# Reordering the queries, the scores and the FFN scaling in a fused Perceiver block: first the second half of the queries, then scores and scaling in alternation

## The chip, the cores and the metric

The kernel runs on one core of one Trainium2 chip. The metric is the device time of one execution in microseconds (us); the median of several executions counts. The work is spread over TensorE (PE in the profile, its weight loads PEld), VectorE (DVE), ScalarE (ACT), GpSimd (POOL) and SyncE (SP, which here only issues transfers). Each engine works through its own instructions in the order in which they are written and waits on semaphores for what other engines produce.

## What is computed

The reference takes `x` (16 x 64 x 1024) and a context (16 x 1024 x 1024) through three stages, each with a residual sum:

```python
x = x + matmul(fake_quant(layernorm(x)), fake_quant(ctx_4096))     # 1: quantized product
x = x + attention(layernorm(x), Wqkv, Wo)    # 2: 32 query heads of 32, one k/v head, ALiBi, causal
x = x + ffn(layernorm(x), weight, bias, gate_w, in_channel_scale, out_channel_scale)   # 3

# attention
scores = jnp.einsum('bqhd,bkd->bhqk', q, k) * scale
probs = softmax(where(causal, scores + alibi, NEG_INF))
attn = jnp.einsum('bhqk,bkd->bqhd', probs, v) @ Wo
# ffn
routing = softmax(xf @ gate_w.T)
in_scale, out_scale = routing @ in_channel_scale, routing @ out_channel_scale
out = xf * in_scale @ sign(weight).T * out_scale + bias
```

## The kernel before

The 1024 rows of `x` are cut into eight tiles of 128 rows, each of which holds two batches of 64 rows. The three stages overlap between tiles: in step i, TensorE works on stage 1 of tile i+1, the queries and scores of tile i, the attention product and projection of tile i-1, and the FFN of tile i-1 and then i-2. The whole order is written out by hand, engine by engine, in `first_half(s)` and `second_half(s)`, which `run_steps` calls for each step (L132). `s.front` (f), `s.middle` (m) and `s.next` (n) say which tiles exist in a step. Steps 2 to 7 run through the code that the change touches with f and m both true; step 8 has no tile in front.

Products that need precision beyond float16 are made from a high and a low part: ACT makes the high part (`hi_part`), DVE the low part (`lo_part`), and TensorE adds three products. These functions matter here:

- `query(s, n, ks)` on PE makes half n of the transposed queries, 12 matmuls for each k in `ks`; `low` and `high` are k 0 to 3 and 4 to 7. When the last k of half 1 is done, ACT runs `q_hi(s, 1)` and DVE then `q_lo(s, 1)` (writes qT_lo, L830).
- `scores(s, b)` on PE (L1393, 24 matmuls for each batch b) waits for both `q_lo`. DVE's `scores_in(t, h, b)` (L982) scales one 128x512 block of them, adds ALiBi and writes `Pr`; `row_max` (L987) and `subtract_max` (L316) follow. For b = 1 the subtraction is on POOL, for b = 0 on DVE. The first four of these calls were the function `softmax_in`, at the end of the second half; the rest, `softmax_rest`, begins the next step's first half with `scores_in(m, 1, 0)`.
- The router's weights come out of `router_probs` (DVE) through `router_t` (PE, L1467) and `rt_copy` (ACT). `inscale(s, c)` (PE, L1479, 4 matmuls each) spreads them over half c of the channels. DVE's `xs(s, c)` (L1068) multiplies the FFN's input by them, ACT's `xs_hi` and DVE's `xs_lo` (XS_lo, L828) split it.
- `context(t, pair)` on PE (L1308) is a quarter of stage 1: 8 matmuls with a branch (L1318) in their middle.
- `outscale(s, n)` (PE, L1496) opens the FFN's half in the next step. Its guards are the waits

```python
emptied(Step(s.i - 1), f"is{n}")                  # xs_lo(n) of the step before is done
e.wait_ge(s_stt, (s.i - 1) * 4 + 2 + n)           # n=0: two scores_in are done, n=1: three
```

so that `outscale(s, 0)` needs `xs_lo(0)` and `scores_in(0, 1)`, and `outscale(s, 1)` needs `xs_lo(1)` and `scores_in(1, 0)`. `ffn(s, n, ks)` (L1504) follows each. ACT's `outscale_copy` (L554) waits for `outscale(s, 1)`; behind it on ACT stand the exponentials `exp` (L548), for which the transposes `pt` (PE, L1327) wait.

Of the kernel before, what the change touches and what calls it, by code (L numbers as in the profile page):

```python
# [145 lines left out]
def build(nc, x, context, wqkv, wo, w_t, bias, quant_in, small_in, scales_in, alibi, out):  # L146
    ctx = ExitStack()
    with ctx:
# [672 lines left out]
        def _(e):  # L821
# [241 lines left out]
            def xs(s, c):  # L1063

                m, bank, sl = s.i - 1, s.bank(f"is{c}"), slice(4 * c, 4 * c + 4)
                e.wait_ge(s_is, m * 2 + c + 1)
                rows = ln2T[:, sl, :].rearrange("p k t -> p (k t)")
                e.scalar_tensor_tensor(rows, T[:, bank, :], C_XS, rows, ALU.mult, ALU.mult)\  # L1068
                    .then_inc(s_xs, 1)

            def xs_lo(s, c):
                m, bank, sl = s.i - 1, s.bank(f"is{c}"), slice(4 * c, 4 * c + 4)
                e.wait_ge(s_xshi, m * 2 + c + 1)
                lo_part(XS[1][:, sl, :], ln2T[:, sl, :], XS[0][:, sl, :], 1.0, s_free[bank])
# [10 lines left out]
            def softmax_in(m):  # L1085

                scores_in(m, 0, 0)
                scores_in(m, 0, 1)
                row_max(m, 0, 0)
                subtract_max(e, m, 0, 0)  # L1090
# [32 lines left out]
            def entry():  # L1123
                stats0(0)
                norm0(0, tok)
                stats0(1)
                norm0(1, tok)
                scales_by_part()
# [72 lines left out]
            def second_half(s):  # L1201
                f, m, n = s.front, s.middle, s.next
                if s.is_step(-1):
                    return entry()
                if s.is_step(0):
                    return step_0(s)
                if s.is_step(1):
                    return step_1(s, Step(2))
                if f and not s.is_step(2):
                    x1(s)  # L1210
                if m and not s.is_step(2):
                    ta_lo(s, 1)
                if f and not s.is_step(2):
                    norm1(s)
                if n and not s.is_step(2):
                    stats0(s.i + 1)
                if m and not s.is_step(2):
                    x2(s, 0)
                if f and not s.is_step(2):
                    t1_lo(s, 0)  # L1220
                    t1_lo(s, 1)
                if m and not s.is_step(2):
                    x2(s, 1)
                if f:
                    v_lo(s)

                def second_norm():
                    if m:
                        norm2(s)

                if n and not s.is_step(2):
                    norm0(s.i + 1, tok, second_norm)
                else:
                    second_norm()
                if f:
                    q_lo(s, 0)
                    k_lo(s)
                if m:
                    router_max(s)
                    router_probs(s)  # L1240
                if m:
                    xs(s, 0)
                    xs(s, 1)
                if f:
                    q_lo(s, 1)
                if m:
                    xs_lo(s, 0)
                    xs_lo(s, 1)
                if f:
                    softmax_in(s.i)  # L1250

            run_steps(first_half, second_half)

# [2 lines left out]
        def _(e):  # L1256
# [5 lines left out]
            low, high = range(KT // 2), range(KT // 2, KT)  # L1262
# [27 lines left out]
            def context(t, pair, s=None):  # L1290


                if pair == 0:
                    if t < 2:
                        emptied(s, "T0")
                    else:
                        e.wait_ge(s_aT, 16 * (t - 1))
                    if t == 2:
                        e.wait_ge(s_x2, 2)
                    at_least(e, s_k, t)  # L1300
                    at_least(e, s_v, t)
                c = 2 * pair + 1
                e.wait_ge(s_rf[c % RING], uses(t, c) + 1)

                def products(k, lhs, first, last):
                    for n in range(2):
                        for b in range(2):
                            ins = e.matmul(C[b * S:(b + 1) * S, n, :], lhs(b),  # L1308
                                           b16[:, (2 * pair + b) % BRING, k, n * HALF:(n + 1) * HALF],
                                           start=first, stop=last)  # L1310
                    return ins

                def rows(k):
                    return lambda b: aT[:, 2 * pair + k, b * S:(b + 1) * S]

                products(0, rows(0), pair == 0, False)

                with e.If_ne(uneven, 0):  # L1318
                    for k in range(2):
                        for part in range(3):  # L1320
                            products(k, lambda b: zfrac[:, part, :], False, False)
                products(1, rows(1), False, pair == 3).then_inc(s_ctx, 1)
# [27 lines left out]
            def query(s, n, ks=range(KT)):  # L1350

                if n == 0 and k_low(ks):
                    if s.is_step(1):
                        e.wait_ge(s_k, 2)
                        e.wait_ge(s_v, 2)
                    else:
                        at_least(e, s_an, s.i * 4)
                if s.is_step(2) and k_low(ks):
                    e.wait_ge(s_fe, n + 1)
                for k in ks:  # L1360
                    rows = [t[:, k, :].rearrange("p (b t) -> p b t", b=2) for t in T16]
                    for g in range(4):
                        dst = query_to(s.i, n).rearrange("p (b g t) -> p g b t", b=2, t=S)[:, g]
                        at = (4 * n + g) * P
                        hi, lo = (w[:, k, at:at + P] for w in Wqkv)
                        e.matmul(dst, hi, rows[0], start=k == 0 and g == 0, stop=False,  # L1366
                                 skip_group_check=True)
                        e.matmul(dst, hi, rows[1], start=False, stop=False, skip_group_check=True)  # L1368
                        last = e.matmul(dst, lo, rows[0], start=False, stop=k == KT - 1,  # L1369
                                        skip_group_check=True)  # L1370
                if ks[-1] == KT - 1:
                    last.then_inc(s_qT, 1)
# [98 lines left out]
            def inscale(s, c):  # L1471
                bank = bank_for(s, f"is{c}")
                if c == 0:
                    emptied(s, "rT")
                    if s.is_step(1):
                        e.wait_ge(s_prep, 3)
                for k in range(4):
                    at = (4 * c + k) * P
                    last = e.matmul(T[:, bank, k * P:(k + 1) * P], insc[:, at:at + P], rT[:, :],  # L1479
                                    start=True, stop=True)  # L1480
                last.then_inc(s_is, 1)
# [143 lines left out]
            def second_half(s):  # L1625
                f, m, n = s.front, s.middle, s.next
                if s.is_step(-1):
                    return entry(s)
                if s.is_step(0):
                    return step_0(s)  # L1630
                if s.is_step(1):
                    return step_1(s, Step(2))
                if f and not s.is_step(2):
                    t1(s)
                if m and not s.is_step(2):
                    project(s, 1, high)
                if f:
                    kv(s)
                    query(s, 0)
                if m:  # L1640
                    t2(s)
                if f:
                    query(s, 1, low[:1])
                    tk(s)
                    query(s, 1, low[1:])
                if m:
                    router(s)
                if f:
                    query(s, 1, high[:2])
                if n:  # L1650
                    context(s.i + 1, 0, s)
                if m:
                    router_t(s)
                if f:
                    query(s, 1, high[2:3])
                if m:
                    inscale(s, 0)
                    inscale(s, 1)
                if f:
                    query(s, 1, high[3:])  # L1660
                if n:
                    context(s.i + 1, 1)
                if f:
                    scores(s, 0)
                    scores(s, 1)
# [45 lines left out]
```

## Time and profile before

| | |
|---|---|
| runs of the kernel | 442.26, 444.58 and 444.25 us, median 444.25 us |
| profiled execution | 442.26 us, of which the span from first to last instruction is 440.5 us |
| PE busy | 373.2 us (85%) |
| DVE busy | 309.6 us (70%) |
| ACT busy | 257.3 us (58%) |
| POOL busy | 96.2 us (22%) |

A busy share alone doesn't say which engine bounds the kernel: the shares are means over a start-up of some 110 us in which transfers count, six steps that repeat, and a tail with little left to overlap. The rows below come from the repeating steps, where the changed lines run.

### The profile page before, as it was taken

How to read it: one execution, taken by the hardware profiler on the slowest of the kernel's cores; microseconds unless marked ns; L12 is line 12 of the kernel's file. 1: busy time of each engine (PE TensorE's matmuls, PEld its weight loads, DVE VectorE, ACT ScalarE, POOL GpSimd, SP SyncE). 2: the span in 40 equal slices, each digit the busy share in tenths (PEclk: the TensorE clock that was granted, in tenths of full speed). 3: DMA queues.
4: the chain of work that ended last, by engine and by line, in shares of the span. 5: the costliest groups of instructions: out<-in, count | busy, mean ns of one | idle time of the engine just before them, and what ended most of it. 6: DMA issues, size and time to landing. Idle time of an engine off the chain costs nothing.

```text
span 440.5 us, 9600 instructions
## 1 busy us (share of the span) xinstructions
PE 373.2 (85%) x3952; PEld 255.0 (58%) x3952; DVE 309.6 (70%) x586; ACT 257.3 (58%) x308; POOL 96.2 (22%) x116
## 2 busy tenths in 40 slices
PE   0444956996999999998999999989999999899565
PEld 0114835953636956694659655965587558755432
DVE  7668579989846387787688688858786865483331
ACT  4777898747678655764666576756577523241110
POOL 5210010003503203140314041403231312031202
PEclk9955997999899999999999999999999999999759
DMA  7999998699399864777277736774591010001001
GB/s 313 390 399 409 409 378 325 241 361 357 134 388 305 285 235 136 258 235 251 76 283 243 218 131 254 270 217 144 199 328 25 1 49 2 3 1 49 0 0 48
DMA packets 30097, 91.97 MB, mean 209 GB/s; under 512 B 8224, under 2 KB 8224, under 8 KB 30048
## 3 DMA queue, kind: packets, MB, share of 16 engines
q1 hardware_dynamic: 27888, 83.40, 53.5%
q10 hardware_dynamic: 2160, 7.87, 4.8%
q8 instruction: 37, 0.61, 0.5%
q14 instruction: 12, 0.10, 0.1%
HBM read 85.50 MB, written 4.19 MB: 204 GB/s over the span
## 4 chain that ended last, share of the span: by engine, by line
PE 65%; DVE 11%; DMA 9%; ACT 5%; issue 4%; SPq 3%; POOL 0%; POOLq 0%; DVEq 0%; ACTq 0%
PE R L1504 13%; PE T L1327 7%; PE R L1278 7%; DMA ring<-ctx 7%; PE R L1280 6%; PE R L1279 6%; PE C L1308 5%; PE R L1366 4%; PE R L1369 4%; PE R L1368 4%; ACT b L524 3%; PE T L1460 3%; SPq L348 2%; PE R L1393 2%; DVE st L878 1%
## 5 line engine op out<-in xcount | busy, mean ns | idle before, releaser
L524 ACT ACTIVATE b<-ring,quant,qpar 128x2048 uint8<-128x2048 f32 x64 | 133.0, 2091 | 10.7 <-DMA ring<-ctx 7.9
L1366 PE MATMUL R<-T_hi,Wqkv_hi 128*128 128x128 f16 x448 | 78.6, 221 | 0.0
L1368 PE MATMUL R<-T_lo,Wqkv_hi 128*128 128x128 f16 x448 | 78.5, 221 | 0.0
L1369 PE MATMUL R<-T_hi,Wqkv_lo 128*128 128x128 f16 x448 | 78.4, 221 | 0.0
L1504 PE MATMUL R<-sgn,XS_hi 128*128 128x512 fp8e4 x128 | 49.7, 388 | 0.0
L1308 PE MATMUL C<-b,aT 128*64 128x512 f16 x256 | 37.2, 416 | 14.5 <-ACT b L524 10.7
L1504 PE MATMUL R<-sgn,XS_lo 128*128 128x512 fp8e4 x128 | 49.4, 386 | 0.0
L1366 PEld LDWEIGHTS R<-T_hi,Wqkv_hi 128*128 128x128 f16 x448 | 44.8, 100 | 1.0
L1368 PEld LDWEIGHTS R<-T_lo,Wqkv_hi 128*128 128x128 f16 x448 | 44.2, 99 | 0.1
L1369 PEld LDWEIGHTS R<-T_hi,Wqkv_lo 128*128 128x128 f16 x448 | 44.3, 99 | 0.0
L316 POOL TENSOR_TENSOR Pr<-Pr,mx 128x512 f32<-128x512 f32 x16 | 16.7, 1044 | 125.2 <-DVE mx L987 125.2
L1278 PE MATMUL R<-Wo,attT_hi 128*128 128x512 f16 x112 | 43.0, 384 | 0.5 <-DVE attT_lo L1013 0.5
L1279 PE MATMUL R<-Wo,attT_hi 128*128 128x512 f16 x112 | 42.7, 381 | 0.0
L1280 PE MATMUL R<-Wo,attT_lo 128*128 128x512 f16 x112 | 42.7, 381 | 0.0
L878 DVE BATCH_NORM_STATS2 st<-X 128x6 f32<-128x512 f32 x48 | 33.3, 693 | 4.0 <-DMA X<-x 2.5
L425 POOL TENSOR_TENSOR small<-small,consts 128x1 f32<-128x1 f32 x24 | 4.6, 192 | 134.2 <-DVE small L885 134.2
L448 POOL TENSOR_TENSOR X<-X,XL 128x512 f32<-128x512 f32 x16 | 20.3, 1271 | 48.7 <-DVE XL L1082 48.7
L1327 PE MATMUL T<-ident,XL 128*128 128x128 f32 x120 | 19.3, 314 | 12.1 <-DVE XL L890 12.1
L1308 PEld LDWEIGHTS C<-b,aT 128*64 128x64 f16 x256 | 12.4, 115 | 28.6 <-ACT b L524 13.7
L573 ACT ACTIVATE attT_hi<-T 128x512 f16<-128x512 f32 x16 | 9.5, 594 | 31.6 <-PE T L1327 31.6
L828 DVE TENSOR_TENSOR PT_lo<-T,PT_hi 128x512 f16<-128x512 f32 x32 | 20.6, 684 | 8.6 <-ACT PT_hi L508 8.6
L1327 PEld LDWEIGHTS T<-ident,XL 128*128 128x128 f32 x120 | 16.0, 163 | 14.9 <-DVE XL L890 13.7
(145 smaller groups left out, 873.1 us busy)
## 6 DMA issues: line engine op xcount, KB each, us to landing
ring<-ctx SPq DMA_DIRECT2D x64, 1024.0 KB, 6.2
ring<-L_attn_Wo SPq DMA_DIRECT2D x4, 1024.0 KB, 7.6
ring<-L_ffn_weight SPq DMA_DIRECT2D x4, 1024.0 KB, 5.0
out<-X ACTq DMA_DIRECT2D x8, 512.0 KB, 2.6
Wo<-L_attn_Wqkv SPq DMA_DIRECT2D x7, 544.0 KB, 15.1
X<-x ACTq DMA_DIRECT2D x7, 512.0 KB, 4.0
sgn<-L_attn_Wqkv SPq DMA_DIRECT2D x1, 544.0 KB, 18.1
X<-x SPq DMA_DIRECT2D x1, 512.0 KB, 12.8
```

The costliest lines, as they stand in the source:

```text
L524: e.activation(b8[:, c % BRING, :], ring[:, slot, :], ACT.Identity, scale=qR2, bias=qZ2).then_inc(s_rf[slot], 1)
L828: e.tensor_tensor(dst, src, hi, ALU.subtract).then_inc(done, 1)
L878: link(e.bn_stats(st[k][:, h, :], src[:, h * HALF:(h + 1) * HALF]))
L1278: e.matmul(dst, lhs[0], rhs[0], start=first, stop=False)
L1279: e.matmul(dst, lhs[0], rhs[1], start=False, stop=False)
L1280: return e.matmul(dst, lhs[1], rhs[0], start=False, stop=last)
L1308: ins = e.matmul(C[b * S:(b + 1) * S, n, :], lhs(b), b16[:, (2 * pair + b) % BRING, k, n * HALF:(n + 1) * HALF], start=first, stop=last)
L1327: last = e.transpose(T[:, bank, n * P:(n + 1) * P], src, ident[:, :])
L1366: e.matmul(dst, hi, rows[0], start=k == 0 and g == 0, stop=False, skip_group_check=True)
L1368: e.matmul(dst, hi, rows[1], start=False, stop=False, skip_group_check=True)
L1369: last = e.matmul(dst, lo, rows[0], start=False, stop=k == KT - 1, skip_group_check=True)
L1504: last = e.matmul(R[:, 2 + n, :], XS[part][:, k, :], sgn[:, k, n * HALF:(n + 1) * HALF], start=k == 0 and part == 0, stop=k == KT - 1 and ...
```

## The change

On DVE, in the second half of a step, `q_lo(s, 1)` moves ahead of both `xs`, and the calls of `xs`, `xs_lo` and the four of `softmax_in` are put in alternation. On PE the last query group is joined to the one before it, so that it runs ahead of `inscale`, and `context(s.i + 1, 1)` goes between the two `inscale`. No instruction is added or taken away, and ACT, POOL and SP keep their order.

```diff
@@ DVE, second_half
                 if m:
                     router_max(s)
                     router_probs(s)
+                if f:
+                    q_lo(s, 1)
                 if m:
                     xs(s, 0)
+                if f:
+                    scores_in(s.i, 0, 0)
+                if m:
                     xs(s, 1)
                 if f:
-                    q_lo(s, 1)
+                    scores_in(s.i, 0, 1)
                 if m:
                     xs_lo(s, 0)
+                if f:
+                    row_max(s.i, 0, 0)
+                if m:
                     xs_lo(s, 1)
                 if f:
-                    softmax_in(s.i)
+                    subtract_max(e, s.i, 0, 0)
@@ PE, second_half
                 if m:
                     router_t(s)
                 if f:
-                    query(s, 1, high[2:3])
+                    query(s, 1, high[2:])
                 if m:
                     inscale(s, 0)
-                    inscale(s, 1)
-                if f:
-                    query(s, 1, high[3:])
                 if n:
                     context(s.i + 1, 1)
+                if m:
+                    inscale(s, 1)
                 if f:
                     scores(s, 0)
                     scores(s, 1)
```

On DVE, from the end of the router's work in step 3 up to the third `scores_in` of the next half, the kernel before has (ln2T is written by `xs`, qT_lo by `q_lo`, XS_lo by `xs_lo`, Pr<-R by `scores_in`, mx by `row_max`, Pr<-Pr by `subtract_max`):

```order
L1060 TENSOR_TENSOR rstack<-rt,rstack 128x16
L1068 SCALAR_TENSOR_TENSOR ln2T<-T,ln2T 128x512 x2
L830 SCALAR_TENSOR_TENSOR qT_lo<-R,qT_hi 128x2x256
L828 TENSOR_TENSOR XS_lo<-ln2T,XS_hi 128x512 x2
L982 SCALAR_TENSOR_TENSOR Pr<-R,alibi_sb 128x512 x2
L987 TENSOR_REDUCE mx<-Pr 128x8
L316 TENSOR_TENSOR Pr<-Pr,mx 128x512
L982 SCALAR_TENSOR_TENSOR Pr<-R,alibi_sb 128x512
```

On DVE at the same place the changed kernel has:

```order
L1060 TENSOR_TENSOR rstack<-rt,rstack 128x16
L830 SCALAR_TENSOR_TENSOR qT_lo<-R,qT_hi 128x2x256
L1068 SCALAR_TENSOR_TENSOR ln2T<-T,ln2T 128x512
L982 SCALAR_TENSOR_TENSOR Pr<-R,alibi_sb 128x512
L1068 SCALAR_TENSOR_TENSOR ln2T<-T,ln2T 128x512
L982 SCALAR_TENSOR_TENSOR Pr<-R,alibi_sb 128x512
L828 TENSOR_TENSOR XS_lo<-ln2T,XS_hi 128x512
L987 TENSOR_REDUCE mx<-Pr 128x8
L828 TENSOR_TENSOR XS_lo<-ln2T,XS_hi 128x512
L316 TENSOR_TENSOR Pr<-Pr,mx 128x512
L982 SCALAR_TENSOR_TENSOR Pr<-R,alibi_sb 128x512
```

The two `xs` now stand behind `q_lo`, and the first `xs_lo` behind both `scores_in` of the first pair, while it stood ahead of them.

On PE the kernel before has, from the last matmuls of the query's last group in step 3 to the first of the scores (a branch leaps over the row of 24):

```order
L1368 MATMUL R<-T_lo,Wqkv_hi 128x2x64
L1369 MATMUL R<-T_hi,Wqkv_lo 128x2x64
L1308 MATMUL C<-b,aT 64x512 x4
L1318 COMPARE_AND_BRANCH
L1308 MATMUL C<-b,zfrac 64x512 x24
L1318 UNCONDITIONAL_BRANCH
L1308 MATMUL C<-b,aT 64x512 x4
L1393 MATMUL R<-kbd_hi,qT_hi 128x128 x2
```

On PE the changed kernel has there (its lines stand 8 lower in the file; L1487 is `inscale`, L1401 the scores):

```order
L1376 MATMUL R<-T_lo,Wqkv_hi 128x2x64
L1377 MATMUL R<-T_hi,Wqkv_lo 128x2x64
L1487 MATMUL T<-rT,scales 128x128 x4
L1316 MATMUL C<-b,aT 64x512 x4
L1326 COMPARE_AND_BRANCH
L1316 MATMUL C<-b,zfrac 64x512 x24
L1326 UNCONDITIONAL_BRANCH
L1316 MATMUL C<-b,aT 64x512 x4
L1487 MATMUL T<-rT,scales 128x128 x4
L1401 MATMUL R<-kbd_hi,qT_hi 128x128 x2
```

The eight matmuls of `inscale`, which stood together ahead of the query's last group, now follow it, four on each side of the context group.

## Rows read from the trace of the kernel before

**Rows 1.** The page, part 1: busy us (share of the span) and instructions by engine.

```profile
PE 373.2 (85%) x3952; PEld 255.0 (58%) x3952; DVE 309.6 (70%) x586; ACT 257.3 (58%) x308; POOL 96.2 (22%) x116
```

**Rows 2.** Windows: stretch, length, busy us by engine, granted clock, DMA share, GB/s.

```profile
154.32:199.19 44.87, 44.17 (x495) 30.64 (x493) 35.89 (x69) 28.69 (x37) 11.62 (x12) 1.00 0.65 219
199.19:245.13 45.94, 44.35 (x495) 30.53 (x493) 35.89 (x69) 28.68 (x37) 11.61 (x12) 1.00 0.63 212
...
384.15:390.00 5.85, 4.92 (x63) 2.71 (x64) 5.82 (x10) 1.06 (x2) 0.96 (x1) 1.00 0.02 4
```

**Rows 3.** Timeline, PE, step 4: start us, us, engine, line, tiles, [idle before].

```profile
246.07 0.61 PE L1479 MATMUL T<-rT,scales 32*128 32x128 f16 x8
246.62 0.23 PE L1366 MATMUL R<-T_hi,Wqkv_hi 128*128 128x128 f16 x1
...
247.24 0.22 PE L1369 MATMUL R<-T_hi,Wqkv_lo 128*128 128x128 f16 x1
247.39 0.41 PE L1308 MATMUL C<-b,aT 128*64 128x512 f16 x2
...
248.92 0.23 PE L1393 MATMUL R<-kbd_hi,qT_hi 64*128 64x128 f16 x2 [0.47 <-issue]
...
250.37 0.41 PE L1308 MATMUL C<-b,aT 128*64 128x512 f16 x2
...
251.36 0.37 PE L1496 MATMUL R<-scales,rT 32*128 32x512 f16 x1
...
253.50 0.39 PE L1496 MATMUL R<-scales,rT 32*128 32x512 f16 x1
...
255.56 0.51 PE L1327 MATMUL T<-ident,Pr 128*128 128x128 f32 x3
```

**Rows 4.** Timeline, DVE, the same stretch of step 4.

```profile
248.13 0.69 DVE L830 SCALAR_TENSOR_TENSOR qT_lo<-R,qT_hi 128x512 f16<-128x512 f32 x1 [0.34 <-ACT qT_hi L508]
248.73 1.28 DVE L828 TENSOR_TENSOR XS_lo<-ln2T,XS_hi 128x512 f16<-128x512 f32 x2
...
249.93 1.28 DVE L982 SCALAR_TENSOR_TENSOR Pr<-R,alibi_sb 128x512 f32<-128x512 f32 x2
...
252.45 0.69 DVE L982 SCALAR_TENSOR_TENSOR Pr<-R,alibi_sb 128x512 f32<-128x512 f32 x1
```

**Rows 5.** Timeline, ACT and then POOL, the same stretch.

```profile
247.50 0.60 ACT L508 ACTIVATE qT_hi<-R 128x512 f16<-128x512 f32 x1 [1.76 <-PE R L1369]
...
253.92 1.02 ACT L554 ACTIVATE XL<-R 128x1024 f32<-128x1024 f32 x1 [2.81 <-PE R L1496]
254.84 1.14 ACT L548 ACTIVATE Pr<-Pr 128x512 f32<-128x512 f32 x2
...
253.81 1.04 POOL L316 TENSOR_TENSOR Pr<-Pr,mx 128x512 f32<-128x512 f32 x1 [11.37 <-DVE mx L987]
```

**Rows 6.** Timeline, step 0: first scores on PE, first `scores_in` on DVE.

```profile
56.28 0.23 PE L1393 MATMUL R<-kbd_hi,qT_hi 64*128 64x128 f16 x2 [1.50 <-DVE qT_lo L830]
...
57.17 0.69 DVE L982 SCALAR_TENSOR_TENSOR Pr<-R,alibi_sb 128x512 f32<-128x512 f32 x1 [0.24 <-PE R L1393]
```

**Rows 7.** Timeline, PE and then DVE, step 7, which has no context product.

```profile
384.15 0.23 PE L1393 MATMUL R<-kbd_hi,qT_hi 64*128 64x128 f16 x2 [1.46 <-issue]
...
386.60 0.37 PE L1496 MATMUL R<-scales,rT 32*128 32x512 f16 x1 [0.93 <-DVE Pr L982]
...
385.17 1.28 DVE L982 SCALAR_TENSOR_TENSOR Pr<-R,alibi_sb 128x512 f32<-128x512 f32 x2
```

**Rows 8.** Timeline, PE, step 3, and the branches of that stretch (durations in ns).

```profile
205.93 0.62 PE L1308 MATMUL C<-b,aT 128*64 128x512 f16 x4 [0.88 <-issue]
...
208.63 0.39 PE L1496 MATMUL R<-scales,rT 32*128 32x512 f16 x1
...
L1318 PEldq COMPARE_BRANCH  x3: 205/207/2022, 197.4 to 203.9; - x3
```

**Rows 9.** Timeline, PE, step 5: first context product after the transposing transfer.

```profile
289.96 0.41 PE L1308 MATMUL C<-b,aT 128*64 128x512 f16 x2 [0.88 <-DMA aT<-a]
```

More of the change, by code:

```diff
@@ L1240, in second_half @@
                     router_probs(s)
-                if m:
-                    xs(s, 0)
-                    xs(s, 1)
                 if f:
@@ L1246, in second_half @@
                 if m:
+                    xs(s, 0)
+                if f:
+                    scores_in(s.i, 0, 0)
+                if m:
+                    xs(s, 1)
+                if f:
+                    scores_in(s.i, 0, 1)
+                if m:
                     xs_lo(s, 0)
+                if f:
+                    row_max(s.i, 0, 0)
+                if m:
                     xs_lo(s, 1)
                 if f:
-                    softmax_in(s.i)
+                    subtract_max(e, s.i, 0, 0)
             run_steps(first_half, second_half)
@@ L1654, in second_half @@
                 if f:
-                    query(s, 1, high[2:3])
+                    query(s, 1, high[2:])
                 if m:
                     inscale(s, 0)
-                    inscale(s, 1)
-                if f:
-                    query(s, 1, high[3:])
                 if n:
                     context(s.i + 1, 1)
+                if m:
+                    inscale(s, 1)
                 if f:
```

## The prediction, made before the changed kernel was run

> **What bounds the kernel now.** I read the page's busy shares first: PE 85%, the next engine 70% [rows 1]. A mean doesn't name a limit, so I cut the trace into stretches from one `router_t` to the next. In step 2 to 3 PE is busy 44.17 of 44.87 us at a granted clock of 1.00, that is its upper level of 2.4 GHz, and DVE 35.89 [rows 2]. So in the repeating steps TensorE sets the pace, and a change counts only by what it does to the moments at which PE waits. The timeline of PE shows them for step 4 [rows 3]: the only sizeable one is the 0.47 us before the scores at 248.92. The other thing to see is where PE is almost late for nothing. `outscale(0)` starts at 251.36, just as the context group before it (0.99 us from 250.37) runs out, but DVE's second `scores_in`, which it also needs, ends at 249.93 + 1.28 = 251.21 [rows 3, 4]. That guard is 0.15 us from costing something. In step 7, where there is no context group between, the same guard does bite: 0.93 us of idle PE before `outscale(0)`, released by DVE [rows 7]. The guard of `outscale(1)` (the third `scores_in`, end 252.45 + 0.69 = 253.14) has 0.36 us to its start at 253.50 [rows 3, 4]. DVE is thus a second, nearly equal chain between the queries' end and `outscale(1)`, and the change lengthens exactly that chain.
>
> **Part 1, PE: the queries end earlier.** The last twelve matmuls no longer wait behind eight of `inscale`, which take 246.62 - 246.07 = 0.55 us with their step over to the query; joining two groups of twelve also saves a step over: (247.24 - 246.62)/11 = 0.056 us for one, 0.68 us for twelve, against 247.39 - 246.62 = 0.77 with the change of group [rows 3]. I take 0.55 + 0.1 = 0.65 us in all. `q_hi` follows on ACT (idle for 1.76 us before it, so free), then `q_lo` on DVE, 248.13 before [rows 4, 5]; DVE is idle there too, since `xs` now stands behind. So `q_lo` starts at 247.47 and ends at 248.16. PE has the same work as before between router and scores and arrives without a wait at 248.92 - 0.47 - 0.1 = about 248.3. Of the wait at the scores nothing is left: a gain of 0.6 to 0.65 us in each of six steps, 3.8 us if nothing else moved. In step 7, PE still waits (1.46 us before, about 1.0 now), and also starts the scores 0.65 us earlier [rows 7].
>
> **Part 2, DVE: the chain behind `q_lo`.** Before, both `xs` ran in the time in which DVE waited for `q_hi`. That time was their cover, and it is gone: DVE now waits idle for `q_hi`, and 2 x 0.60 us of work comes after. One such instruction behind another starts 0.60 us later (two of XS_lo: 248.73 to 249.93) [rows 4]. The first `scores_in` also has to wait for all 24 matmuls of batch 0; in step 0, where DVE really waited for them, it started 57.17 - 56.28 = 0.89 us after the first of them [rows 6]. Now the chain of step 4, by starts: `q_lo` 247.47, `xs(0)` 248.07, then idle until 248.3 + 0.89 = 249.2, `scores_in(0,0)` 249.2, `xs(1)` 249.8, `scores_in(0,1)` 250.4, `xs_lo(0)` 251.0, `row_max` 251.6, `xs_lo(1)` 252.2, `subtract_max` 252.8, and the next half's `scores_in(1,0)` 253.4, which ends at 254.08. ACT's two `xs_hi` (0.6 us each) fit between: each has over 1.2 us from the end of its `xs` to its `xs_lo`.
>
> **Part 3, the guards.** `outscale(0)` now waits for `xs_lo(0)`, which ends at 251.0 + 0.68 = 251.68; with the 0.15 us that DVE's end takes to reach PE (386.45 to 386.60 in step 7, where 386.45 is two `scores_in` behind 385.17) it starts at 251.8, where it started at 251.36. PE itself would be there at 250.7, so it idles 1.1 us. `outscale(1)` would follow 253.50 - 251.36 = 2.14 us later [rows 3], at 253.97, but its guard opens at 254.08 + 0.15 = 254.2: 0.7 us later than 253.50. So the 0.65 us won at the scores are already inside this number, and the step stands 0.7 us behind.
>
> **Who waits behind it.** Behind `outscale(1)`, PE has eight matmuls and then the transpose `pt` at 255.56, which the exponential of 254.84 released (first half ends about 255.46) [rows 3, 5]. ACT's copy and exponentials start at `outscale(1)` + 0.42, and shift by the same 0.7. The subtraction on POOL ended at 254.85 and was needed at 255.36; it shifts by 0.95 (with `scores_in(1,0)`, 252.45 to 253.4) against 0.7, and keeps 0.25 us. ACT's conversion behind `xs_hi(1)` runs some 2 us later, into time in which ACT idled 2.81 us [rows 5]. Ring slots come free as much later, with loads that a whole step separates from their use. In the whole of the stretch from step 2 to 3 PE is idle for 44.87 - 44.17 = 0.70 us [rows 2], and two thirds of that are the wait at the scores; what is left for the other forty microseconds is some 0.2 us, and DVE's and ACT's work there starts from PE's. So nothing gives the 0.7 back. Even the wait for the transposing transfer in step 5 (0.88 us) [rows 9] stays: its source is made by DVE behind PE's work of the same step.
>
> **Sum.** Steps 2, 4, 5, 6 and 7 look alike; step 7 by its own rows: `outscale(1)` at 388.73 becomes 389.4. That is 5 x 0.7 = 3.5 us. Step 3 is different. There PE lost 0.88 us inside the context group at 205.93, on a branch that took 2022 ns where others take 207 [rows 8], and `outscale(1)` stood at 208.63. DVE's chain there is step 4's less 45.94 us, the time from one `router_t` to the next [rows 2], so its guard opens at 254.2 - 45.94 = 208.3, and the branch's loss falls into the new idle time: a gain of 0.35 us. Total 3.5 - 0.35 = +3.1 us. Against the profiled execution, 442.26 us (1.76 us of it outside the span), that is 445.4. That execution was the fastest of three, the median is 444.25, so I forecast 447.3.
>
> **A rule on the branch.** The row says 0.88 us of idle PE at one branch of three [rows 8]. The Trainium skill, "Runtime: NRT & Kernel Launch", section "Instruction fetch mechanics", holds that a taken branch out of the fetched window waits for a fetch. By the rule the position of a branch in PE's stream matters; `context(i+1, 1)` moves by four matmuls here. Apart from that sentence: the same loss at a new place costs 0.88 us, ahead of the scores, where it isn't covered in full. I keep it for the upper end.
>
> **The rivals.**
> (a) *The guards don't bite; the kernel gets faster.* Then only part 1 is left: 6 x 0.65 = -3.9 us, 440.4. The point that decides is whether `scores_in(1,0)` has ended by the time that PE reaches `outscale(1)`, at about 252.9; my chain has it end 1.2 us later. For it speaks that the scores are read as soon as they are there; against it that ten DVE instructions follow the query's end where eight did. 0.07.
> (b) *The guards bite less: about no change.* If DVE starts its `scores_in` earlier or reaches PE faster, each step loses 0.3 instead of 0.7: 5 x 0.3 - 0.75 = +0.8, 445.0. The lower end of the part is +0 and the upper +2.2. 0.20.
> (c) *More than the guards is late.* The POOL subtraction has 0.25 us left, and a branch may stall anew: 3.1 + 0.9 to 3.1 + 6 x 0.3, 448.2 to 449.2. 0.10.
> (d) *Each DVE instruction starts only when the one before has ended.* The chain has nine starts behind `q_lo`; at 0.68 instead of 0.60 us they give 0.7 us more, 6 steps +4.2, 451.5. The rows speak against it: XS_lo's successor starts 0.08 us before XS_lo ends [rows 4]. 0.03. The Trainium skill, "VectorE: DVE Perf Modes", section "The DRAIN you can't avoid", states such a wait for an empty pipeline; the trace doesn't agree for these shapes.
> The clock is no rival: with idle stretches of 1.46 and 0.93 us in step 7 it stayed at 1.00 [rows 2, 7].
>
> **How the numbers follow.** The forecast, +2.2 to +4 us, has 0.60, (a) 0.07, (b) 0.20, (c) 0.10, (d) 0.03. 0.5%, about what a measurement of this kernel can tell from no change, is 2.2 us. Slower by more: the forecast, (c) and (d), 0.73; within: (b), 0.20; faster: 0.07. The runs before spread over 2.3 us, so the range goes from (b)'s middle less 1 us, 444.0, to (c)'s upper end plus 0.8, 450.0.
>
> **What would show it.** After: no wait before the scores in steps 2 to 6; DVE idle before `q_lo`, with `xs` behind it; about 1.1 us of idle PE before `outscale(0)`, released by XS_lo, and 0.2 us before `outscale(1)`; periods of about 45.55 us where 44.87 stood. I am wrong if PE reaches `outscale(1)` without idling, or if a later part of the step has idle time that takes the delay up.

## The result and the profile after

The changed kernel takes 445.95 us in the median of 20 runs (443.68 to 449.0), the kernel before 441.87 us in the median of 20 (439.57 to 445.66). The ratio is 1.0093, with a 95% interval of 1.0074 to 1.0113: 3.3 to 5.0 us slower, about 4.1. The median of the first three runs of the kernel before, which the prediction had, lay higher (444.25 us) than that of the twenty; the ratio is the number to hold against its +3.1 us (0.7%).

The profiled execution took 443.82 us, with a span of 442.0; it was among the fastest of its kernel. The page hardly shows the change: against [rows 1] PE's busy time fell by 0.4 us and DVE's by 1.0, and ACT's rose by 0.9.

```profile
PE 372.8 (84%) x3952; PEld 255.0 (58%) x3952; DVE 308.6 (70%) x586; ACT 258.2 (58%) x308; POOL 96.0 (22%) x116
```

The stretch from `router_t` of step 2 to that of step 3, as a window of the changed kernel, is the one to compare with the first of [rows 2]:

```profile
154.07:199.71 45.64, 44.21 (x495) 30.61 (x493) 35.80 (x69) 28.89 (x37) 11.60 (x12) 1.00 0.63 213
```

It lasts 45.64 us where 44.87 stood, 0.77 us more. PE's busy time is nearly the same (44.21 for 44.17 us) at the same clock, so 0.73 us of it is new idle time. The next three stretches last 45.64 us too. PE's timeline of step 4 shows where it is (`inscale` is L1487 here, the context L1316, the scores L1401, `outscale` L1504, `pt` L1335). `router_t` starts at 245.35, so 0.22 us are to be taken off to compare with [rows 3]:

```profile
246.96 0.39 PE L1487 MATMUL T<-rT,scales 32*128 32x128 f16 x4
247.28 1.05 PE L1316 MATMUL C<-b,aT 128*64 128x512 f16 x8
248.26 0.39 PE L1487 MATMUL T<-rT,scales 32*128 32x128 f16 x4
248.59 0.23 PE L1401 MATMUL R<-kbd_hi,qT_hi 64*128 64x128 f16 x2
...
250.03 1.05 PE L1316 MATMUL C<-b,aT 128*64 128x512 f16 x8
...
252.02 0.38 PE L1504 MATMUL R<-scales,rT 32*128 32x512 f16 x1 [0.93 <-DVE XS_lo L828]
...
254.50 0.37 PE L1504 MATMUL R<-scales,rT 32*128 32x512 f16 x1 [0.27 <-DVE Pr L982]
```

The wait before the scores is gone. They start at 248.59 - 0.22 = 248.37, where they started at 248.92. But 0.93 us now stand before `outscale(0)`, released by `xs_lo(0)`, and 0.27 us before `outscale(1)`, released by the third `scores_in`. DVE's timeline of the same stretch, against [rows 4]:

```profile
247.69 0.69 DVE L830 SCALAR_TENSOR_TENSOR qT_lo<-R,qT_hi 128x512 f16<-128x512 f32 x1 [2.80 <-ACT qT_hi L508]
248.30 0.68 DVE L1068 SCALAR_TENSOR_TENSOR ln2T<-T,ln2T 128x512 f32<-128x512 f32 x1
249.47 0.69 DVE L982 SCALAR_TENSOR_TENSOR Pr<-R,alibi_sb 128x512 f32<-128x512 f32 x1 [0.50 <-PE R L1401]
250.08 0.68 DVE L1068 SCALAR_TENSOR_TENSOR ln2T<-T,ln2T 128x512 f32<-128x512 f32 x1
250.68 0.68 DVE L982 SCALAR_TENSOR_TENSOR Pr<-R,alibi_sb 128x512 f32<-128x512 f32 x1
251.28 0.68 DVE L828 TENSOR_TENSOR XS_lo<-ln2T,XS_hi 128x512 f16<-128x512 f32 x1
251.88 0.68 DVE L987 TENSOR_REDUCE mx<-Pr 128x8 f32<-128x512 f32 x1
252.47 0.68 DVE L828 TENSOR_TENSOR XS_lo<-ln2T,XS_hi 128x512 f16<-128x512 f32 x1
253.07 0.69 DVE L316 TENSOR_TENSOR Pr<-Pr,mx 128x512 f32<-128x512 f32 x1
253.67 0.68 DVE L982 SCALAR_TENSOR_TENSOR Pr<-R,alibi_sb 128x512 f32<-128x512 f32 x1
```

DVE idles for 2.80 us before `q_lo`, in the time in which it did both `xs` before. Then it works without a break, but for 0.50 us of waiting for the scores, and PE waits for it twice.

### The profile page after: what moved, and what is told of

It reads as the page before. It is cut to its first block, busy times and chain, and to the rows that moved or that the text cites. A ratio compares the mean times of both kernels' runs of the same rounds, so it can differ in the third digit from the quotient of the medians.

```text
span 442.0 us, 9600 instructions
## 1 busy us (share of the span) xinstructions
PE 372.8 (84%) x3952; PEld 255.0 (58%) x3952; DVE 308.6 (70%) x586; ACT 258.2 (58%) x308; POOL 96.0 (22%) x116
## 4 chain that ended last, share of the span: by engine, by line
PE 62%; DVE 16%; DMA 8%; ACT 5%; issue 5%; SPq 3%; POOL 0%; POOLq 0%; DVEq 0%; ACTq 0%
PE R L1512 10%; DMA ring<-ctx 7%; PE T L1335 7%; PE R L1286 7%; PE R L1287 6%; PE R L1288 6%; PE R L1374 5%; PE R L1377 5%; PE R L1376 5%; PE C L1316 4%; PE T L1468 4%; ACT b L524 3%; SPq L348 2%; DVE Pr L982 2%; DVE Wo L830 1%
## 5 line engine op out<-in xcount | busy, mean ns | idle before, releaser
L1316 PE MATMUL C<-b,aT 128*64 128x512 f16 x256 | 37.8, 423 | 13.2 <-ACT b L524 11.2
L830 DVE SCALAR_TENSOR_TENSOR qT_lo<-R,qT_hi 128x512 f16<-128x512 f32 x14 | 9.7, 692 | 28.3 <-ACT qT_hi L508 28.2
L1316 PEld LDWEIGHTS C<-b,aT 128*64 128x64 f16 x256 | 12.6, 116 | 27.3 <-ACT b L524 14.2
L1335 PE MATMUL T<-ident,XL 128*128 128x128 f32 x120 | 17.8, 297 | 11.2 <-DVE XL L890 11.2
```

The source lines that it names most:

```text
L1316: ins = e.matmul(C[b * S:(b + 1) * S, n, :], lhs(b), b16[:, (2 * pair + b) % BRING, k, n * HALF:(n + 1) * HALF], start=first, stop=last)
L1335: last = e.transpose(T[:, bank, n * P:(n + 1) * P], src, ident[:, :])
```

## The experiments

Theory: DVE's chain from the end of the queries to `xs_lo` and the third `scores_in` opens the guards of both `outscale`, and the change made it longer than PE's own way. Rivals: PE's new order or the branch in the context group costs the time; one of the two parts costs it alone; something else is late behind the guards.

Ratios are against runs of the kernel before on the same chip. "Period" is the time from the `router_t` of step 2 to that of step 3 in each kernel's trace, which repeats to 0.02 us where no transfer or branch disturbs it.

| kernel | period, us | ratio, 95% interval |
|---|---|---|
| before | 44.87 | 1 |
| the change | 45.64 | 1.0093 [1.0074, 1.0113] |
| PE's order alone | 45.81 | 1.0121 [1.0079, 1.0163], second timing |
| DVE's order alone | 46.18 | 1.0207 [1.0159, 1.0255] |
| the change, short `xs_lo` | 44.85 | 0.9999 [0.9967, 1.0031] |
| PE's order, DVE's order by the guards | 44.81 | 0.9971 [0.9946, 0.9996] |
| the same with a split guard | 44.59 | 0.9958 [0.9930, 0.9987] |
| PE's order, both `xs` first, `xs_lo` on POOL | 44.43 | 0.9919 [0.9882, 0.9957] |
| the change, `xs_lo` on POOL | 45.09 | 0.9981 [0.9959, 1.0003] |
| before, `xs_lo` on POOL | 44.87 | 1.0003 [0.9968, 1.0038] |

**Each part alone.** First the edit of PE without that of DVE:

```diff
@@ DVE, second_half, as in the kernel before
                 if m:
                     xs(s, 0)
                     xs(s, 1)
                 if f:
                     q_lo(s, 1)
```

> Only the order on PE is changed; DVE keeps both xs ahead of q_lo. Theory (DVE's chain from the query's end to outscale(1) sets the pace): xs(1) now waits for the inscale(1) behind the context group, q_lo stands behind it, so q_lo ends some 1.0 us later than before, the scores start about 1.0 us later and nothing gives it back: six steps, +6 us, about 448 against 442, ratio 1.013 to 1.014. Rival (the earlier end of the queries is worth 0.65 us by itself, the loss is DVE's order alone): 6 x 0.65 = 3.9 us faster, ratio 0.991.

Measured at first: 1.0205, with an interval from 1.0138 to 1.0272 out of four runs. The window shows what it costs a step:

```profile
153.75:199.56 45.81, 44.15 (x494) 30.62 (x492) 35.90 (x69) 28.90 (x37) 11.63 (x12) 1.00 0.63 214
```

That is +0.94 us, as expected, and its place is as expected too. In step 4 of this kernel `xs(1)` waits for the `inscale(1)` behind the context group, `q_lo` stands behind it, and the scores wait for 1.43 us where 0.47 stood. DVE's rows, then PE's:

```profile
247.42 0.69 DVE L1068 SCALAR_TENSOR_TENSOR ln2T<-T,ln2T 128x512 f32<-128x512 f32 x1 [2.50 <-PE T L1479]
248.73 0.69 DVE L1068 SCALAR_TENSOR_TENSOR ln2T<-T,ln2T 128x512 f32<-128x512 f32 x1 [0.62 <-PE T L1479]
249.34 0.68 DVE L830 SCALAR_TENSOR_TENSOR qT_lo<-R,qT_hi 128x512 f16<-128x512 f32 x1
...
250.12 0.23 PE L1393 MATMUL R<-kbd_hi,qT_hi 64*128 64x128 f16 x2 [1.43 <-issue]
```

The ratio stood higher than the sum from the trace, so the same kernel was timed once more:

> The order on PE alone, timed once more, since four runs left its ratio between 1.014 and 1.027. From its trace, a period of 45.81 us for 44.87: 5 x 0.94 and some 1.0 in step 7 are 5.7 us, ratio 1.013. Rival (something outside the repeating steps got slower too): 1.02.

Measured: 1.0121 [1.0079, 1.0163], period again 45.81. The two intervals overlap between 1.014 and 1.016. The expected sum of 1.013 lies in the second and just under the first, and the traces show a term that it doesn't have: in both traces of this kernel TensorE's granted clock falls to its lower level, 1.2 GHz, for 6.8 us in step 7, behind a wait of 1.80 us before the scores (1.46 us in the kernel before). The windows, of the first trace and then of the changed kernel at the same place:

```profile
384.00:387.45 3.45, 1.65 (x28) 1.40 (x26) 1.99 (x4) 1.82 (x3) 0.00 (x0) 1.00 0.00 0
...
387.00:395.00 8.00, 6.67 (x58) 3.59 (x58) 7.09 (x12) 0.42 (x1) 1.04 (x1) 0.57 0.01 3
...
386.00:394.00 8.00, 5.82 (x48) 2.91 (x43) 7.92 (x13) 3.24 (x6) 1.04 (x1) 1.00 0.01 3
```

From the `router_t` of step 7 to the end the first trace takes 446.5 - 383.4 = 63.1 us, where the second trace of the kernel before takes 439.4 - 379.1 = 60.3: 2.8 us more. Little of that is the order's: step 7 has no context group, and the scores start 4.01 us behind `router_t` where they started 3.77 us behind it. From the scores to `outscale(1)` PE then takes 7.31 us where it took 4.58, with no longer wait on the way (0.88 us for 0.93): the clock costs about 2.7 us. With 5 x 0.94 and 0.8 us less at a branch (below) that makes 6.7 us, 1.5%, inside both intervals. In the second trace the clock also fell once in step 4, at the end of the 1.43 us before the scores:

```profile
249.70:252.40 2.70, 2.63 (x48) 2.51 (x48) 1.86 (x3) 2.03 (x2) 0.00 (x0) 0.50 0.03 9
```

So the rival had it half: in the repeating steps the mechanism is the theory's, and the price has a second part, the clock's, that the theory didn't foresee. The 1.0 us expected of the order in step 7 isn't there; it is 0.24.

Then the edit of DVE alone, with PE's order as before:

```diff
@@ PE, second_half, as in the kernel before
                 if f:
                     query(s, 1, high[2:3])
                 if m:
                     inscale(s, 0)
                     inscale(s, 1)
                 if f:
                     query(s, 1, high[3:])
```

> Only the order on DVE is changed; PE keeps the query's last group behind inscale. Theory: q_lo and the scores stand where they stood (the 0.47 us wait stays), the two xs follow q_lo, and the third scores_in ends about 0.6 us later than in the full change: outscale(1) some 1.3 us later than before in each of six steps, +8 us, ratio 1.018. Rival (DVE's order costs nothing, the loss is PE's): ratio 1.000.

Measured: 1.0207 [1.0159, 1.0255], period +1.31 us. In its trace the wait before the scores is back at 0.47 us, and the waits before both `outscale` are there with 0.93 and 0.27 us. The clock falls in step 7 here too (0.57 in the mean of 388 to 396 us). But its wait before the scores there is the same as in the kernel before, which kept its upper clock in both traces [rows 7]:

```profile
388.34 0.23 PE L1401 MATMUL R<-kbd_hi,qT_hi 64*128 64x128 f16 x2 [1.46 <-issue]
```

So how long PE waits ahead of it doesn't tell whether the clock falls. Neither part is worth anything by itself. Each lengthens the way from the queries to the guards: PE's edit by holding back `xs(1)` and with it `q_lo`, DVE's by putting both `xs` behind `q_lo`. Together they cost less than either, since DVE's edit frees `q_lo` from `inscale(1)` and PE's brings it forward.

**The chain made shorter.** In the changed kernel the low part of the FFN's input is computed for 16 of 128 columns only, which leaves out part of the computation:

```diff
-                lo_part(XS[1][:, sl, :], ln2T[:, sl, :], XS[0][:, sl, :], 1.0, s_free[bank])
+                cols = slice(0, P) if s.i == 1 else slice(0, 16)
+                lo_part(XS[1][:, sl, cols], ln2T[:, sl, cols], XS[0][:, sl, cols], 1.0, s_free[bank])
```

> The changed kernel, with the low part of the FFN's input (xs_lo) computed from step 2 on for 16 of 128 columns only; the rest of it keeps old values, so part of the computation is left out. No instruction is taken away or moved; two DVE instructions get some 0.45 us shorter each. Theory: the guards open 0.45 and 0.9 us earlier, outscale(1) is 0.7 us earlier in each of six steps: all of the loss is gone, time as the kernel before or 0.5 us under it, ratio 0.998 to 1.000; the idle time before outscale(1) is gone, some 0.5 us stay before outscale(0). Rival (the loss is in PE's new order or in the branch): the loss stays, ratio 1.009.

Measured: 0.9999 [0.9967, 1.0031], period 44.85. The order on PE, the branches and the number of instructions are those of the change; only two DVE instructions a step got shorter, and the loss in the period is gone. (The 0.8 us of the branch told of below would put the ratio at 0.998, inside the interval.) The row of `outscale(0)` in step 4 shows what is left of the wait (`outscale` is L1505 in this kernel; no wait stands before `outscale(1)`):

```profile
250.31 0.38 PE L1505 MATMUL R<-scales,rT 32*128 32x512 f16 x1 [0.46 <-DVE XS_lo L828]
```

**DVE's order by what the guards need.** PE's order is that of the change; DVE does what a guard waits for first. The edit of the second half is shown; the first half of the next step does the rest of `softmax_rest`, without the two calls that moved here:

```diff
                 if f:
                     q_lo(s, 1)
                 if m:
                     xs(s, 0)
-                if f:
-                    scores_in(s.i, 0, 0)
-                if m:
                     xs(s, 1)
                 if f:
-                    scores_in(s.i, 0, 1)
+                    scores_in(s.i, 0, 0)
                 if m:
                     xs_lo(s, 0)
                 if f:
-                    row_max(s.i, 0, 0)
+                    scores_in(s.i, 0, 1)
                 if m:
                     xs_lo(s, 1)
                 if f:
+                    scores_in(s.i, 1, 0)
+                    row_max(s.i, 0, 0)
+                    row_max(s.i, 0, 1)
                     subtract_max(e, s.i, 0, 0)
```

> PE's order as in the changed kernel; DVE's order serves the guards: q_lo, xs(0), xs(1), scores_in(0,0), xs_lo(0), scores_in(0,1), xs_lo(1), scores_in(1,0), then the row maxima and the subtraction. Theory: scores_in(0,1) ends at 251.15 on step 4's clock of the trace before, outscale(0) starts at 251.3 and outscale(1) at 253.45, where 251.36 and 253.50 stood: no loss and no gain, ratio 0.999 to 1.000, with some 0.5 us of idle PE before outscale(0) and none before outscale(1). Rival (the loss comes from PE's order): ratio 1.009.

Measured: 0.9971 [0.9946, 0.9996]. This is no loss but, if anything, 1 us of gain, of which the branch told of below is 0.8: the 0.77 us are gone without a shorter instruction or one fewer, by order alone. In step 4:

```profile
250.00 0.37 PE L1507 MATMUL R<-scales,rT 32*128 32x512 f16 x1 [0.43 <-DVE Pr L982]
```

In the next kernel the guard on the second `scores_in` stands where its bank is written:

```diff
-                    e.wait_ge(s_stt, (s.i - 1) * 4 + 2 + n)
+                    e.wait_ge(s_stt, (s.i - 1) * 4 + 1 + 2 * n)
...
             def ffn(s, n, ks):
+                if s.middle and not s.is_step(2) and n == 0 and k_low(ks):
+                    e.wait_ge(s_stt, (s.i - 1) * 4 + 2)
                 for k in ks:
```

> As the last, and the guard on the second scores_in is moved from outscale(0), which doesn't write that bank, to the first FFN product, which does. Theory: outscale(0) hides 0.3 us of the wait: 0.3 to 0.4 us less in each of six steps than the kernel before, 2 us, ratio 0.995 to 0.996. Rival (something else is late once the guards aren't: POOL's subtraction, the exponentials): ratio 1.000.

Measured: 0.9958 [0.9930, 0.9987], period 44.59, 0.28 us under the kernel before, a little less than the 0.3 to 0.4 forecast. The time alone can't tell it from the last kernel; the period can (44.81 and 44.59).

**The low parts on POOL.** POOL idled for 11.37 us before its first subtraction of a step [rows 5]. In steps 2 to 7 it takes over `xs_lo`, behind `with_row_sum`; PE's order is that of the change. The lines for DVE show what it runs in these steps against the kernel before:

```diff
@@ POOL, second_half
+                if s.middle and s.front:
+                    xs_lo(s, 0)
+                    xs_lo(s, 1)
@@ DVE, second_half, steps 2 to 7
+                q_lo(s, 1)
                 xs(s, 0)
                 xs(s, 1)
-                q_lo(s, 1)
-                xs_lo(s, 0)
-                xs_lo(s, 1)
                 softmax_in(s.i)
```

> PE's order as in the changed kernel; xs_lo of steps 2 to 7 is done by POOL, which idles there, and DVE runs q_lo, xs(0), xs(1), then the scores' instructions as the kernel before. Theory: DVE's chain to scores_in(1,0) is two instructions shorter, no guard bites, and the 0.65 us won at the scores stay in each of six steps, plus what step 7 idled before: 4 to 4.5 us faster than the kernel before, ratio 0.990 to 0.991. Rival (POOL's 128x512 subtraction of 1.04 us or its latency opens outscale(1) too late, or it slows DVE): ratio 0.995 to 1.005.

Measured: 0.9919 [0.9882, 0.9957], 3.6 us faster than the kernel before and the fastest of all. In the window no more than 0.29 us of PE's time is idle:

```profile
154.49:198.92 44.43, 44.14 (x495) 30.62 (x493) 35.04 (x67) 28.86 (x37) 13.87 (x14) 1.00 0.64 220
```

Here a gain arrives at last: 44.87 - 44.43 = 0.44 us a step, which is nearly the 0.47 us that PE waited before the scores. It isn't the 0.65 us by which `q_lo` is earlier, since PE had no more than its own wait to win, and `outscale(1)` still waits for 0.06 us. In step 7 both the scores and `outscale(0)` still wait (0.91 and 0.93 us), the second now for POOL's `xs_lo`, so the rival has a part there, and the 3.6 us stay under the 4 to 4.5 expected. Of the 3.6, 0.8 are the branch's (below).

Is the help DVE's relief or the new order? The kernel before with `xs_lo` on POOL and no other edit:

> The kernel before with xs_lo of steps 2 to 7 on POOL and nothing else. Theory: in steps 2 to 6 no guard bit, and the 0.47 us before the scores don't hang on xs_lo, so nothing changes there; only step 7's 0.93 us go: ratio 0.998 to 0.999. Rival (relieving DVE is worth something by itself): ratio 0.993 or lower.

Measured: 1.0003 [0.9968, 1.0038], period 44.87. Relieving DVE by itself is worth nothing that this can tell. The wait in step 7 that was to go stays, with 0.87 us for 0.93: the second `scores_in` ends it, and the first of the pair had waited for the scores. And the changed kernel, its alternation kept, with `xs_lo` on POOL:

> The changed kernel as it is, DVE's alternation of xs and scores_in included, with xs_lo of steps 2 to 7 on POOL. Theory (the place of each DVE instruction behind the query's end counts, not their number alone): scores_in(0,1) still stands behind xs(1) and ends at 251.1 on step 4's clock of the trace before, so outscale(0) starts at 251.25 where 250.7 would be possible, 0.1 us ahead of the kernel before: period 44.75, ratio 0.996 to 0.998, slower than the kernel with both xs first (44.43, 0.992). Rival (only the number of DVE instructions counts): the same as that kernel, period 44.4, ratio 0.992.

Measured: 0.9981 [0.9959, 1.0003], period 45.09. It is slower than the kernel with both `xs` first, so the place of each instruction counts, not only the number: `outscale(0)` waits for 0.42 us for the second `scores_in`, which stands behind `xs(1)`. But it is also 0.3 us a period slower than forecast. (Its period is 0.22 us over that of the kernel before and its time no longer, since the branch's 0.8 us, below, are gone here too.) The trace names most of the excess: `outscale(1)` waits for 0.24 us for the third `scores_in`, because the subtraction ahead of it took 1.22 us where it takes 0.69 elsewhere. It ran while POOL was busy with the second `xs_lo`. DVE's rows of step 4, then POOL's:

```profile
250.65 1.22 DVE L316 TENSOR_TENSOR Pr<-Pr,mx 128x512 f32<-128x512 f32 x1
251.80 0.68 DVE L991 SCALAR_TENSOR_TENSOR Pr<-R,alibi_sb 128x512 f32<-128x512 f32 x1
...
250.17 1.16 POOL L476 TENSOR_TENSOR XS_lo<-ln2T,XS_hi 128x512 f16<-128x512 f32 x1 [0.62 <-ACT XS_hi L517]
```

**The stalls that the forecast took as fixed.** A second trace of the kernel before, unedited:

> The kernel before once more, for a second trace. The prediction took two idle stretches of PE as fixed parts of the step: 0.88 us at a branch in step 3 and 0.88 us for the transposing transfer in step 5. If they belong to the program they stand at the same places; if they come and go with the run, at others or nowhere. Everything else, among it the 0.47 us before the scores, stays.

Measured: 441.17 us. The wait for the transposing transfer in step 5 isn't in this trace; it comes and goes with the run (8 of the 12 traces of this study have it, always in step 5 and always with 0.82 to 0.90 us). The stall at the branch stands at its old place, with another length:

```profile
204.63 0.62 PE L1308 MATMUL C<-b,aT 128*64 128x512 f16 x4
205.60 0.62 PE L1308 MATMUL C<-b,aT 128*64 128x512 f16 x4 [0.34 <-issue]
```

All four traces with PE's old order have it (0.88, 0.34, 0.34 and 0.60 us, the branch itself 2022, 1482, 1482 and 1742 ns). None of the eight traces with the new order has it. There the slowest of the three branches of that stretch, the same one, took 323 ns in the changed kernel:

```profile
L1326 PEldq COMPARE_BRANCH  x3: 205/207/323, 197.9 to 203.8; - x3
```

So the loss at this branch went with the order on PE. The period tells what it cost, which is more than the idle time in the row: from the `router_t` of step 3 to that of step 4 the kernel before takes 45.94 and 45.40 us in its two traces, and with `xs_lo` on POOL 45.66, against 44.87 in the step ahead. That is 1.07, 0.53 and 0.79 us, 0.8 in the mean. Why this branch and not another stays open: it is the one in the context group behind the scores, and 73 matmuls stand between `router_t` and it in either order, so its own place didn't change.

With DVE's order alone the stall was there and cost nothing: that period is 46.19 us, like its neighbour of 46.18. The wait before `outscale(0)` was shorter by as much, 0.39 us where 0.93 stands in its other steps:

```profile
205.45 0.62 PE L1316 MATMUL C<-b,aT 128*64 128x512 f16 x4 [0.34 <-issue]
206.46 0.38 PE L1504 MATMUL R<-scales,rT 32*128 32x512 f16 x1 [0.39 <-DVE XS_lo L828]
```

## Why the prediction was right, and where it was off

**The bound.** That PE paces the repeating steps, and that DVE's chain to the guards of `outscale` was nearly as long, held: [rows 3, 4 and 7] said so, and two shorter DVE instructions took the whole loss of the period away.

**The queries' gain.** Forecast 0.65 us earlier at `q_lo`; it starts at 247.69 - 0.22 = 247.47, to the hundredth the forecast. The scores start at 248.37, where I had put 248.3. The small miss is a term that I left out: two `inscale` groups of four take 0.32 + 0.33 us against 0.55 for one of eight, 0.1 us more. So PE gains 0.55 us and not 0.6 to 0.65.

**DVE's chain.** Forecast `scores_in(0,0)` at 249.2, `xs_lo(0)` at 251.0, `scores_in(1,0)` at 253.4. Measured, less 0.22: 249.25, 251.06, 253.45. One instruction started 0.59 to 0.61 us behind another in every pair, so rival (d), with its 0.68, is out. (Seven starts follow `scores_in(0,0)`, so it would have cost 0.56 us and not 0.7.) The Trainium skill, "VectorE: DVE Perf Modes", section "The DRAIN you can't avoid", states a wait for the empty pipeline, but in the same place says that a next instruction that isn't held starts earlier. The prediction left that exception out; the rows fit it.

**The guards.** Forecast `outscale(0)` at 251.8 and `outscale(1)` at 254.2; measured 251.80 and 254.28. Idle PE: forecast 1.1 and 0.2 us, measured 0.93 and 0.27; the first is smaller because PE arrives later by the term above. The loss of a step, forecast 0.7 us, is 0.77 us in the periods and, in step 7 from `router_t` to `outscale(1)`, 9.03 us against 8.35, 0.68 us.

**Nothing gives it back, in the periods.** The only wait of the rest of a period is 0.14 us long, as before. POOL's subtraction, for which I had 0.25 us left, was not waited for. The clock stayed at 1.00 through the repeating steps, as forecast, though step 7 of the changed kernel idles for 1.91 us before `outscale(0)`. That the clock was "no rival" went too far all the same: with DVE's order alone it fell behind the very 1.46 us that I had named.

In the trace of the changed kernel the 0.68 us of step 7 are given back. They are still there at the transposes of step 8, which start 34.19 us behind the `router_t` of step 7 where they started 33.52 us behind it. But the clock, which falls in step 8 in every trace, fell ahead of them in the kernel before and behind them here. The kernel before, then the changed one:

```profile
413.90 1.97 PE L1327 MATMUL T<-ident,XL 128*128 128x128 f32 x8 [3.75 <-DVE XL L890]
...
416.15 1.09 PE L1335 MATMUL T<-ident,XL 128*128 128x128 f32 x8 [3.75 <-DVE XL L890]
```

So from the `router_t` of step 7 to the end both take 60.0 to 60.3 us. Two other traces have the 1.09 us too (the split guard, and the change with `xs_lo` on POOL) and nine have the 1.97. Whether the change has a part in this isn't shown.

**Step 3, right in size by another way.** I let the stall at the branch fall into the new idle time, which made step 3 a gain of 0.35 us and the sum 3.1. Against that very trace the gain is 45.94 - 45.64 = 0.30 us. But the stall didn't fall into the idle time, it was gone, and step 3 waits for 0.93 and 0.27 us like the others. That such a stall can be hidden there is what DVE's order alone shows. And its length was one draw: in the mean of three traces it costs 0.8 us and not 1.07, so step 3 is about even.

The sum is then 5 x 0.77 + 0.68 = 4.5 us, less 0.8 at the branch: 3.7 us, against 4.1 [3.3, 5.0] measured. The traces themselves give less, since the 0.68 came back: from the `router_t` of step 2 to the end the changed kernel takes 3.1 us more than the second trace of the kernel before. The waits that come and go, for the transposing transfer and with the clock, are of the size of what is left; no run splits it further. The first of these I had forecast to stay, and it isn't in the trace of the changed kernel, nor in the second of the kernel before.

The rule of the Trainium skill, "Runtime: NRT & Kernel Launch", section "Instruction fetch mechanics", has the place of a taken branch's target in the instruction stream decide whether it waits for a fetch. The prediction applied it to the group ahead of the scores, which the change moves. The branch that stalled is in the group behind them, whose place didn't move, so the place alone doesn't account for the stall's going, and whether a fetch was its cause isn't shown.

**The median.** 447.3 rested on the median of three runs, 444.25. With twenty the kernel before stands at 441.87, so the absolute number was 2.4 us too high by the sample and 1.0 us too low by the difference. That the two offset each other in part, and 447.3 came within 1.4 us of 445.95, is luck.

## What to carry to other kernels

A wait that is filled on the bounding engine is worth something only up to the next guard: here the 0.55 us won before the scores came back as 1.2 us of waiting at the next two guards. Before moving an instruction out of the shadow of a wait (`xs` before `q_lo`), list each guard that the bounding engine meets afterwards, and count what stands ahead of the instruction that opens it; then order the helper engine by these guards, not by the data flow. The edit on PE and `q_lo` ahead of both `xs` were sound as a start: with the low parts on an idle engine, and `xs` not put in alternation with the scores' instructions, they are worth 0.8%, 0.2% of which is the branch's.

## What the runs showed of the hardware that was not expected

A DVE subtraction of 128x512 float32 with both inputs in on-chip memory took 0.69 us alone and 1.08 to 1.22 us where it overlapped POOL's `xs_lo` (1.15 to 1.17 us), in all twelve cases of the two kernels. In each it ended 0.55 us after POOL's instruction had. DVE's other instructions kept their 0.67 to 0.69 us under the same overlap: `scores_in` and `xs`, which read one input from the matmul's result memory, and `row_max`, which reads a single input from on-chip memory. In the fastest kernel, step 4, DVE and then POOL:

```profile
249.45 1.09 DVE L316 TENSOR_TENSOR Pr<-Pr,mx 128x512 f32<-128x512 f32 x1
...
247.71 2.29 POOL L476 TENSOR_TENSOR XS_lo<-ln2T,XS_hi 128x512 f16<-128x512 f32 x2 [7.06 <-ACT XS_hi L517]
```

The granted clock fell in step 7 in three of the twelve traces: both of PE's order alone, and DVE's order alone. PE's waits don't tell these from the others. DVE's order alone had waited 1.46 us before the scores, as both traces of the kernel before had, which kept their clock, and the changed kernel kept it through 0.91 and 1.91 us. What decides isn't shown. The price is shown: about 2.7 us in the first trace of PE's order alone. In step 8, whether eight transposes ran at the lower or the upper level made 0.8 us, and that too differed from trace to trace.

And a stall of PE at one branch, in one place, appeared in all four traces with one order of the instructions ahead of it and in none of the eight with another, though as many matmuls stood ahead of it.
